# Two remainder products on different halves of the array's rows, and a deviation made ahead of two maxima, in a fused state-space and attention kernel

## The reference

```python
y = ys[:, 0] + ys[:, 2, :, ::-1] + ...            # four scans, summed: [B, 192, 4096]
y = _ln_cf(y, out_norm_w, out_norm_b)             # over the 192 channels of a point
y = y * silu(z)
x1 = x + einsum('cd,bdhw->bchw', out_proj_w, y)   # 192 x 192
# second layer, on x1
g_x, theta_x, phi_x = conv1x1(x1, g), conv1x1(x1, theta), conv1x1(x1, phi)   # 96 channels each
f = softmax(einsum('bon,bom->bnm', theta_x, phi_x), axis=-1)
out = conv1x1(einsum('bnm,bom->bon', f, g_x), W) + x1
```

## Time and profile before

| | |
|---|---|
| median of 3 runs | 9250.66 us (9244.29 to 9259.2) |
| profiled execution | 9256.15 us, its span 9254.4 us |
| mean granted TensorE clock | 0.981 |
| busy: PE, PEld | 8642.6 us (93%), 4648.4 us (50%) |
| busy: DVE | 7377.0 us (80%) |
| busy: ACT | 6091.9 us (66%) |
| busy: POOL | 3295.4 us (36%) |
| mix of the last image | 8683 to 8790 us |

### The profile page before, as it was taken

How to read it: one execution, slowest core, us unless ns; L and a number is a source line. 1 busy time by engine, 2 the same in 40 slices (tenths; PEclk the granted TensorE clock), 3 DMA queues, 4 the chain that set the end, 5 groups by cost and what they waited for, 6 DMA issues and landing times. The chain is left out here.

```text
span 9254.4 us, 103902 instructions
## 1 busy us (share of the span) xinstructions
PE 8642.6 (93%) x26448; PEld 4648.4 (50%) x26448; DVE 7377.0 (80%) x8229; ACT 6091.9 (66%) x7440; POOL 3295.4 (36%) x1853
## 2 busy tenths in 40 slices
PE   7899998999989998899988999889998899988999
PEld 3336743367433674336733367333673336733476
DVE  6987779877798777987679876798767987689876
ACT  6765677656776567765677556775567755677566
POOL 2870028600286002860038600385003850038400
PEclk9999999999999999999999999999999999999999
DMA  1320013200132001320013200232002320023200
GB/s 53 111 87 13 10 56 112 80 13 10 57 111 82 11 11 59 115 76 10 11 63 111 76 10 11 65 116 71 8 12 68 111 73 8 11 72 114 66 8 12
DMA packets 286693, 503.21 MB, mean 54 GB/s; under 512 B 142155, under 2 KB 143215, under 8 KB 253431
## 3 DMA queue, kind: packets, MB, share of 16 engines
q1 hardware_dynamic: 286199, 497.81, 17.9%
HBM read 467.99 MB, written 29.47 MB: 54 GB/s over the span
## 5 line engine op out<-in xcount | busy, mean ns | idle before, releaser
L1400 DVE TENSOR_TENSOR pl<-pf,ph 128x1024 fp32r<-128x1024 f32 x1024 | 1254.3, 1225 | 1007.1 <-ACT ph L1020 999.5
L1253 DVE TENSOR_TENSOR_SCAN h<-ps,h,dbu 128x512 f32<-128x512 f32 x1536 | 1884.2, 1267 | 59.8 <-POOL dbu L1087 29.9
L1087 POOL TENSOR_TENSOR dbu<-bs,du 128x1024 f32<-128x1024 f32 x768 | 1808.1, 2369 | 54.1 <-POOL du L1078 54.1
L1020 ACT ACTIVATE ph<-pf 128x1024 fp32r<-128x1024 f32 x1024 | 1085.3, 1060 | 750.3 <-PE ps L708 750.0
L885 ACT ACTIVATE ps<-dt,negA 128x512 f32<-128x512 f32 x1536 | 1037.5, 687 | 684.8 <-DVE h L1253 684.8
L1014 ACT ACTIVATE pf<-ps 128x1024 f32<-128x1024 f32 x1024 | 1050.4, 1026 | 530.7 <-PE ps L695 513.3
L1066 POOL MEMSET pad<- 128x66 f32 (+1 forms) x64 | 7.2, 200 | 3853.2 <-DVE fa L1429 3853.0
L1384 DVE TENSOR_REDUCE mx<-ps 128x1 f32<-128x512 f32 x1792 | 1168.6, 683 | 78.8 <-PE ps L606 62.5
L1261 DVE TENSOR_TENSOR hc<-h,ps 128x1024 f32<-128x1024 f32 x768 | 937.9, 1221 | 110.3 <-PE ps L487 19.7
L487 PE MATMUL ps<-xhl,selr 128*128 128x512 f32 x1536 | 768.1, 585 | 238.8 <-DVE hc L1261 238.6
L1072 POOL TENSOR_TENSOR dt<-dt,ze 128x1024 f32<-128x1024 f32 x256 | 604.0, 2359 | 1061.3 <-ACT dt L878 1061.3
(11 more groups left out here) (204 smaller groups left out, 14540.6 us busy)
## 6 DMA issues: line engine op xcount, KB each, us to landing
bs<-rows SPq DMA_DIRECT2D x256, 1024.0 KB, 5.1
bs<-rows SPq DMA_DIRECT2D x512, 256.0 KB, 6.1
xa<-in_x SPq DMA_DIRECT2D x130, 256.0 KB, 2.9
xb<-in_x SPq DMA_DIRECT2D x130, 128.0 KB, 3.0
out<-fa SPq DMA_DIRECT2D x64, 256.0 KB, 2.1
rdb<-rden SPq DMA_DIRECT2D x56, 192.0 KB, 3.4
out<-fa SPq DMA_DIRECT2D x64, 128.0 KB, 2.4
xhl<-ct SPq DMA_DIRECT2D x256, 8.0 KB
```

The costliest lines, as they stand in the source:

```text
L1020: A(ph[:, mp % 2, :, :], pf[:, mp % 2, :, :], ACT.Copy).then_inc(S["ph_ready"], 1)
L1087: pool.tensor_tensor(dbu[:, q, :, :], bs[par][:, q, :, :], du[:, r:r + 1, :].to_broadcast([P, 2, T]), ALU.mult).then_inc(S["dbu_ready"], 1)
L1253: dve.tensor_tensor_scan(h[:, j, ::step], ps[:, 2 + e, ::step], dbu[:, q, e, ::step], h[:, j, end:end + 1], ALU.mult, ALU.add)\
L1400: TT(pl[:, mp % 2, :, :], pf[:, mp % 2, :, :], ph[:, mp % 2, :, :].bitcast(F32), ALU.subtract)\
```

## The change

Four edits, all for the mix.

1. The output products. wo1 gets the remainder's weights in rows 64 to 127 too, by two more loads at the start. ScalarE copies ob's rows 0 to 63 to its rows 64 to 127, once a chunk (the new tile rows are no longer zeroed by GpSimd). TensorE then makes both products with oa first; of the two with ob, that for bank 2 contracts over rows 0 to 63 and that for bank 3 over rows 64 to 127. A new semaphore, twice_ready, counts the copies: the products and VectorE's next deviation wait for it, and the copy waits for gated_ready and for the mixed of the chunk before.
2. TensorE makes tops 0 and 1 ahead of the variance instead of behind it.
3. VectorE makes the deviation of chunk c+1 ahead of the maxima of tops 2 and 3 of the step before, and of their link (`late_tops`), instead of behind them. Steps -1, 0 and 1 have none to pass; in step 7 nothing moves.
4. `run_mix` writes all steps out.

```diff
+                 (wo1[R:P, R:C], w_out[P:C, 0:P]), (wo1[R:P, 0:R], w_out[P:C, P:C]),
...
         def run_mix(eng, step):
-            step(-1, 1, "n")
-            step(0, 0, "np")
-            with eng.Fori(0, (NCH - 4) // 2) as cc:
-                for e in range(2):
-                    step(cc * 2 + (1 + e), (1 + e) % 2, "np")
-            step(NCH - 3, 1, "np")
-            step(NCH - 2, 0, "np")
-            step(NCH - 1, 1, "p")
+            for c in range(-1, NCH):
+                step(c, c % 2, "n" if c < 0 else "np" if c < NCH - 1 else "p")
...
# TensorE
+                    early = "p" in which and not (isinstance(c, int) and c == 0)
                     if "p" in which:
                         pe.wait_ge(S["gated_ready"], i * 2 + 4)
-                        for bank, lo, hi in ((2, R, C), (3, 0, P)):
+                        pe.wait_ge(S["twice_ready"], i + 1)
+                        halves = ((2, R, C, slice(0, R)), (3, 0, P, slice(R, P)))
+                        for bank, lo, hi, _ in halves:
                             mm(ps[:, bank, :], wo0[:, lo:hi], oa[:, :], start=True, stop=False)
-                            m = mm(ps[:, bank, :], wo1[:, lo:hi], ob[:, :], start=False, stop=True)
+                        for bank, lo, hi, at in halves:
+                            m = mm(ps[:, bank, :], wo1[at, lo:hi], ob[at, :], start=False, stop=True)
                         m.then_inc(S["mixed"], 1)
+                    if early:
+                        early_top(c, 0)
+                        early_top(c, 1)
                     if "n" in which:
                         pe.wait_ge(S["sq_ready"], n * 2 + 2)
                         mean_of(1, sqa[:, :], sqb[:, :], "var_ready")
-                    early = "p" in which and not (isinstance(c, int) and c == 0)
-                    if early:
-                        early_top(c, 0)
-                        early_top(c, 1)
...
# ScalarE, at the end of a step
+                    if "n" in which:
+                        act.wait_ge(S["gated_ready"], j * 2 + 4)
+                        if not (isinstance(c, int) and c < 0):
+                            act.wait_ge(S["mixed"], j)
+                        A(ob[R:P, :], ob[0:R, :], ACT.Copy).then_inc(S["twice_ready"], 1)
...
# GpSimd
-                zero_rows(b * 4 + 6, b + 2, (yt[R:P, :, :], sqb[R:P, :], nb_[R:P, :], ob[R:P, :]))
+                zero_rows(b * 3 + 5, b + 2, (yt[R:P, :, :], sqb[R:P, :], nb_[R:P, :]))
...
# VectorE
+                def late_tops(c):
+                    col = 1 + c % 2
+                    early_top(c - 1, 2, col, 6)
+                    early_top(c - 1, 3, col, 7)
+                    dve.wait_ge(S["top_read"], i_0 * NU + c * 4 + 2)
+                    dve.wait_ge(S["mx_link"], i_0 + c)
+                    TT(mx[:, :, 0:1], mx[:, :, 0:1], mx[:, :, col:col + 1], ALU.max).then_inc(S["mx_link"], 1)
...
                     if "n" in which:
                         dve.wait_ge(S["gated_ready"], j * 2 + 2)
+                        if not (isinstance(c, int) and c < 0):
+                            dve.wait_ge(S["twice_ready"], j)
                         deviate(n, pad0[:, bass.ds((c + 1) * T, T)], yt[0:R, 1 - par, :])
+                        if c > 1:
+                            late_tops(c - 1)
                         if not isinstance(c, int) or c + 2 < NCH:
                             add_rem(c + 2, par)
                     if "p" in which:
+                        if c == NCH - 1:
+                            late_tops(c - 1)
```

More of the change, by code:

```diff
@@ L205, in build @@
             "hc_ready", "summed", "y0_added", "y1_added", "zero_h",
-            "yt_ready", "mix_link", "gated_ready", "mixed", "x1_ready", "phi_ready", "phf_ready", "phh_ready", "phl_ready",
+            "yt_ready", "mix_link", "gated_ready", "twice_ready", "mixed", "x1_ready", "phi_ready", "phf_ready", "phh_ready", "phl_ready",
             "gt_ready", "gth_ready", "gtl_ready",
@@ L626, in step @@
                         if isinstance(c, int) and c < 0:
-                            pe.wait_ge(S["rows_zero"], b * 4 + 6)
+                            pe.wait_ge(S["rows_zero"], b * 3 + 5)
                             pe.wait_ge(S["row_one"], b + 2)
                         mm(ps[:, 0, :], avg[:, :], yt[:, q, :], start=False, stop=True).then_inc(S["mean_ready"], 1)
+                    early = "p" in which and not (isinstance(c, int) and c == 0)
                     if "p" in which:
                         pe.wait_ge(S["gated_ready"], i * 2 + 4)
-                        for bank, lo, hi in ((2, R, C), (3, 0, P)):
+                        pe.wait_ge(S["twice_ready"], i + 1)
+                        halves = ((2, R, C, slice(0, R)), (3, 0, P, slice(R, P)))
+                        for bank, lo, hi, _ in halves:
                             mm(ps[:, bank, :], wo0[:, lo:hi], oa[:, :], start=True, stop=False)
-                            m = mm(ps[:, bank, :], wo1[:, lo:hi], ob[:, :], start=False, stop=True)
+                        for bank, lo, hi, at in halves:
+                            m = mm(ps[:, bank, :], wo1[at, lo:hi], ob[at, :], start=False, stop=True)
                         m.then_inc(S["mixed"], 1)
+                    if early:
+                        early_top(c, 0)
+                        early_top(c, 1)
                     if "n" in which:
@@ L1365, in step @@
                            gth[:, gs, 0:O].bitcast(F32), ALU.subtract).then_inc(S["gtl_ready"], 1)
-                        if early:
-                            early_top(c - 1, 2, 1 + par, 6)
-                            early_top(c - 1, 3, 1 + par, 7)
-                            dve.wait_ge(S["top_read"], i_0 * NU + c * 4 + 2)
-                            dve.wait_ge(S["mx_link"], i_0 + c)
-                            TT(mx[:, :, 0:1], mx[:, :, 0:1], mx[:, :, 1 + par:2 + par], ALU.max)\
-                                .then_inc(S["mx_link"], 1)
-                        else:
+                        if c == NCH - 1:
+                            late_tops(c)
+                        if not early:
                             low_theta(i, 0)
```

## The result

| | before | after |
|---|---|---|
| median | 9254.09 us (9244.29 to 9265.56) | 9274.64 us (9262.61 to 9284.47) |
| profiled execution, its span | 9256.15, 9254.4 | 9271.37, 9269.4 |
| eight mixes, VectorE's memset of mx to its nmx | 848.55 | 859.11 |

The ratio is 1.0021, with a 95% interval of 1.0013 to 1.0028: 12 to 26 us slower. The time lies in the range forecast, 12.6 above its centre, and the sign is that of the forecast's sum (+11.4). The line between no change and slower was drawn at 0.2%, 18.5 us. The medians lie 20.6 apart, just beyond it, and the interval holds both sides of it, so these runs don't decide whether the likeliest case ("same") was met.

A forecast was written before the change was run, and what follows sets the result against it. TensorE's sum of work was taken to bound the mix's middle. Per image 0.65 + 0.85 + 1.10 - 3 x 0.09 - 1.04 = +1.29, over eight 10.3, with the start +11.4: 9262 us, range 9244 to 9284.

The forecast's parts named there:

- likeliest case: Whole kernel: a time between 9232 and 9269, within 0.2% of before, given 65%.
- pair of products and visit: TensorE's products with ob: 1.72 becomes 1.29 plus 0.34 for going to 64 rows and back, 0.09 gained a step.
- copy at step 0: ScalarE's copy of ob delays the start of TensorE's products from 8695.89 to 8696.54, +0.65.
- copy at step 1: The copy, behind ScalarE's split of theta, makes TensorE's products start late, +0.85.
- copy at step 7: No mean hides the copy and ob comes later behind phi's start, so the products start late, +1.10.
- three records: The pair on TensorE: only the middle two of four records overlap, 1.29 in all; the forecast case, 50%.
- Rival 2: The pair on TensorE overlaps fully, 0.86 without the visit; kernel 9250, no change; 15%.
- VectorE's second ring: Steps 2 to 6: from mean's end through VectorE's new order and TensorE back to the mean, 11.20 a step.
- lie on each other: Middle steps: VectorE's ring of 11.20 and TensorE's sum of 11.22 coincide; the step was taken as 11.25.
- covered by 0.8: Steps 2 to 6: the copy is through at 4.90 behind the variance, TensorE needs it at 5.70.
- a sign that I am wrong: Products of steps 2 to 6 waiting for the copy would show the prediction wrong.
- Rival 4: TensorE's clock falls at step 0 in the longer wait for the copy, 1.5 an image, +12, 9274; 13%.

The follow-up runs named there:

- same_rows: The changed kernel with both remainder products on rows 0 to 63, no copy, no wait for one, no extra loads; ratio to before 1.0033, 9280.66 us.
- copy_left_out: The changed kernel without the copy of ob and its waits, so its output is not the reference's; ratio to before 0.998, 9228.53 us.
- copy_first: The changed kernel with ScalarE's copy ahead of its wait for phl and of theta's split; ratio to before 1.0004, 9249.15 us.
- after_filled: The changed kernel with unread matmuls in TensorE's waits: two before the first variance, three before step 0's products, one before step 7's; ratio to before 1.0006.
- before_filled: The kernel before with unread matmuls in TensorE's waits: two before the first variance, two before step 0's products; ratio to before 0.9993.
- both_mended: The changed kernel with copy first, waits filled (also before the last tops), and step 1's theta low half behind VectorE's deviation; ratio to before 0.9966, 9222.6 us.
- pair_only: The kernel before with edit 1 alone (pair on two halves, copy, waits, loads), old orders and loop; ratio to before 1.0036, 9282.91 us.

## Why the prediction was right in sum and wrong in its terms

| term, us an image | forecast | measured | by |
|---|---|---|---|
| pair of products and visit, a step | -0.09 | -0.46 | 1.72 to 1.26; same_rows |
| copy at step 0 | +0.65 | +0.6 | step 0 longer by 0.15 with the pair's -0.46 |
| copy at step 1 | +0.85 | +1.0 | step 1 longer by 0.58 with the pair's -0.46 |
| copy at step 7 | +1.10 | +1.8 | steps 6 and 7 longer by 0.9, with two pairs |
| steps 2 to 5 | -0.95 | -1.18 | 45.94 to 44.76 |
| clock | 0 | +0.8 | filled against not filled, 6.5 over 8 |
| all in the mix, eight images | +10.3 | +10.6 | |
| start | +1.1 | +1.3 by its row, +3.9 to the first mix | |

**The pair: the step that failed is "three records".** I took it from records that start in the order of the program, so that the second product's first record would wait for the first product's second. The rows show all four records in 1.13 from first start to last end. The price of the visit was right: 0.34 forecast from the earlier trace rows, 0.39 measured. Rival 2 (full overlap) had the right mechanism for the pair, 0.86 + 0.39, and the wrong time, 9250. "TensorE: Matmul & The Clock Gate", Part 3, of the Trainium skill, says that matmuls on different row groups run together; for whole fp32 products of two records each the trace agrees, with 1.06 for two instead of 1.91.

**The ring: right.** I put VectorE's second ring at 11.20; it takes 11.12, it alone limits the middle, and copy_left_out shows the same 11.12 where no copy is waited for, but 10.87 in step 1, where nothing has been put into the ring. This is why steps 2 to 5 became 1.18 shorter, where TensorE's own sum would have allowed 45.94 - 4 x 10.85 = 2.5. That sum I had put at 11.22, and it is 11.31 - 0.46 = 10.85. Two numbers that "lie on each other" were 0.3 apart, on the side that didn't matter.

**The copy "covered by 0.8" in steps 2 to 6: wrong, without cost.** It rested on the copy following gth and ob. I read the diff's lines for the copy's own waits and not the line above it, where ScalarE waits for phl. The copy starts 0.7 later than I said; it ended at 8734.73, and TensorE took the products up at 8734.88, 0.17 later than right behind the mean. That is a wait for the copy in steps 2 to 6, which I had named as a sign that I am wrong, and about this cover I was. Since VectorE's ring sets the step, it costs nothing. In step 7, where nothing covers it, the same line costs 0.74, and copy_first shows it going: the wait falls from 1.72 to 0.99.

**Step 1.** The copy began 0.65 behind theta's thc (8722.36 to 8723.01), where I had 0.53. The rest of the +0.15 isn't taken apart.

**Rival 4, the clock: it came, in other places than I put it.** I gave 13% to a fall at step 0 in all eight images, 1.5 each. It fell there in three, at waits of 3.31 to 3.36 (the five that held had 3.24 to 3.31; the 2.49 that I gave for before is the last image's, in four images it was 1.28 to 1.48), and at step 7 in five, behind a wait of only 1.72; I didn't ask there at all, though the copy had made a wait where TensorE had none. In return the first variance was low in four images and not in six. Net 6.5 and not 12.

So +10.3 against +10.6 is luck, errors that cancel: the pair and the middle steps gave some 1.7 an image more than forecast, the copy at step 7 and the clock took as much. The case that came is none of the four that I described, but the second's overlap with part of the fourth's clock and a wait that no case had. The measured terms add up to +9.4; the 1.2 up to +10.6 are not placed term by term.

**Outside the mix.** The six weight loads take 3.45 on SyncE's queue where four took 2.16: 1.3, forecast 1.1. The first mix starts 3.9 later. The other 2.6 I can't place, and other kernels without the two loads start as late. By the timed medians after is 20.6 slower (12 to 26 by the interval), by the profiled spans 15.0, by the mixes 10.6. So about half of the measured loss lies outside the mixes, and its cause is open. The filling in the mix doesn't remove it: on one chip after_filled is 12.0 above before_filled, by the mixes 4.0. It is in stages that the change doesn't touch, where the time from one mix to the next moves by up to 9 us between images of one kernel (1037.9 to 1047.0 in both_mended). That the clock's pattern in those stages is what shifts is argued and not shown. The two profiled executions speak rather against it: the mean granted clock was 0.981 before and 0.982 after, though the mixes of after had the lower clock more often.

**Also open:** step 5 of after takes 11.38 to 11.40, 0.26 more than steps 2 to 4, in all images, with VectorE's da waiting 0.88 and not 0.58. It is 2 us over the kernel. copy_first doesn't have it, so it hangs on the late copy, but I didn't isolate the cause.

## What to carry to other kernels

Before costing an instruction that is put into a queue, read what that queue waits for in front of it: its own semaphores are only half of its start time. Making the bounding engine's work shorter pays only as far as the next ring lets it, and where the shorter engine then waits longer at the ends of a stage, the clock can take back what was gained; unread matmuls in those waits are a cheap test of that, and here they shortened the stage too. A total that comes out right says little until its terms are measured one by one.

## What the runs showed of the hardware

- Two fp32 products of 512 columns on different halves of the rows, written A, A, B, B as four records, took as long as one: 1.06 with the entry against 1.91 on one half. One visit from 128 rows to 64 and back cost 0.39.
- The same wait of 2.55 us ahead of the first variance lowered the clock at once in six images of before and during the next product in a seventh, and left it at 2.4 GHz in one; 3.31 at step 0 of after did both, and so did 1.27 ahead of the last tops of before (low in four of eight). The length of one wait doesn't decide it. In after the three images that were low at step 0 had been low at the first variance 8.5 us earlier, and the five others were low at step 7 instead; but in pair_only, behind the same code and waits of 3.30 and 3.31, images 2 and 7 both had the first variance at the full clock, and only image 7 fell at step 0. What decides it isn't shown.
- Four unread products an image (before_filled) or six (after_filled) in waits that were idle anyway kept the clock of every image at 2.4 GHz behind these waits and saved 1.3 and 2.1 us an image.
